# A decoder layer on one core: step order from a table of places, cross units of 4 heads by 256 tokens, and the heads' spreads, stores and broadcasts begun by SyncE

## The reference, cut to what matters

```python
x = x + attn(layernorm(x), w_qkv, w_out)          # window 128: a query chunk sees its own chunk (causal) and the one before
x = x + xattn(layernorm(x), ctx, ctx, mask, ...)  # softmax(q k^T / 4, masked) v, 77 keys for each of 4 sequences
x = x + ffn(layernorm(x), clip_x, clip_down, w_gate, w_up, w_down)   # int8-like rounding, silu(gate) * up, down
```

## Time and profile before

| | us |
|---|---|
| median of 3 runs (lowest, highest) | 945.3 (941.71, 948.7) |
| the profiled execution, its time | 945.94 |
| its span, first to last instruction | 944.2 |
| PE busy / DVE / ACT / POOL | 728.0 / 544.3 / 418.8 / 192.4 |
| granted clock of TensorE, mean | 0.866 |

### The profile page before, as it was taken

One profiled execution on the slowest core, in us unless ns is written; L12 is line 12 of the kernel. 1 busy time (PEld: TensorE's weight loads), 2 busy tenths in 40 slices (PEclk: granted clock), 3 DMA queues, 4 the chain that ended last, 5 costly groups with the idle time before them and its releaser, 6 DMA issues.

```text
span 944.2 us, 13998 instructions
## 1 busy us (share of the span) xinstructions
PE 728.0 (77%) x5008; PEld 412.4 (44%) x5008; DVE 544.3 (58%) x970; ACT 418.8 (44%) x610; POOL 192.4 (20%) x231
## 2 busy tenths in 40 slices
PE   3769888888788997989788778689795684468755
PEld 2446455555545443556445443435343221323344
DVE  4378546665854457566465753345652730559977
ACT  3414544434443544643343455132351342169865
POOL 4002121211321202110231031002002000334536
PEclk9968988899998999999898989688797565679979
DMA  8540141504221344151215413130344012000013
GB/s 258 181 134 3 51 134 42 141 14 115 70 82 30 94 104 109 48 150 48 63 47 134 98 41 86 37 108 14 86 108 130 14 40 45 0 1 1 1 45 134
DMA packets 59187, 71.78 MB, mean 76 GB/s; under 512 B 24635, under 2 KB 36079, under 8 KB 59119
## 3 DMA queue, kind: packets, MB, share of 16 engines
q1 hardware_dynamic: 43792, 50.90, 16.8%
q10 hardware_dynamic: 15327, 19.99, 10.6%
HBM read 17.74 MB, written 4.72 MB: 24 GB/s over the span
## 4 chain that ended last, share of the span: by engine, by line
PE 23%; DVE 12%; issue 6%; DMA 6%; ACT 4%; ACTq 4%; POOL 0%; SPq 0%; POOLq 0%; DVEq 0%
PE banks L676 6%; DMA oc<-sums 4%; PE banks L666 4%; ACTq L906 3%; PE banks L623 2%; PE banks L625 2%; PE banks L549 2%; DVE tops L1280 1%; PE banks L720 1%; PE banks L594 1%; DMA sums<-ls 1%; ACT big L882 1%; PE banks L596 1%; PE banks L653 1%; DVE big L1274 1%
## 5 line engine op out<-in xcount | busy, mean ns | idle before, releaser
L1109 DVE TENSOR_REDUCE mneg<-banks 128x4 f32<-128x1024 f32 (+1 forms) x128 | 145.7, 1152 | 73.8 <-PE banks L587 73.2
L1370 POOL TENSOR_SCALAR_AFFINE_SELECT big<-big 128x512 f32<-128x512 f32 x128 | 85.1, 665 | 448.3 <-ACT big L878 446.9
L878 ACT ACTIVATE big<-banks 128x1024 f32<-128x1024 f32 (+1 forms) x128 | 124.1, 973 | 107.1 <-PE banks L616 74.4
L584 PE MATMUL banks<-big 96*128 96x256 bf16 (+1 forms) x512 | 101.6, 296 | 22.2 <-DVE mneg L1109 9.1
L882 ACT ACTIVATE big<-banks 77x1024 f32<-77x1024 f32 x64 | 64.8, 1019 | 110.7 <-PE banks L625 84.6
L549 PE MATMUL banks<-xnT,weights 128*128 128x512 f32 x192 | 91.7, 607 | 3.0 <-DVE big L1082 1.2
L653 PE MATMUL banks<-big 128*17 128x256 f32 (+1 forms) x1152 | 80.1, 371 | 16.8 <-POOL big L1370 16.7
L1113 DVE TENSOR_REDUCE mneg<-banks 128x8 f32<-128x616 f32 x64 | 49.7, 793 | 68.9 <-PE banks L596 68.7
L616 PE MATMUL banks<-big 99*128 99x256 bf16 (+1 forms) x512 | 76.4, 273 | 9.7 <-ACT big L878 5.6
L587 PE MATMUL banks<-causal,identb 128*128 128x256 bf16 x256 | 77.6, 305 | 0.0
L584 PEld LDWEIGHTS banks<-big 96*128 96x128 bf16 x512 | 51.0, 109 | 58.8 <-issue 28.9
(11 more groups left out here) (150 smaller groups left out, 1165.2 us busy)
## 6 DMA issues: line engine op xcount, KB each, us to landing
big<-parts SPq DMA_DIRECT2D x288, 128.0 KB, 2.5
oc<-sums ACTq DMA_DIRECT2D x16, 512.0 KB
oTs<-oe ACTq DMA_DIRECT2D x64, 64.0 KB, 2.7
out_dram<-oTs SPq DMA_DIRECT2D x16, 256.0 KB, 2.1
xs<-in_x_dram SPq DMA_DIRECT2D x3, 1024.0 KB, 10.1
big<-oe ACTq DMA_DIRECT2D x32, 64.0 KB, 2.9
oTx<-oe ACTq DMA_DIRECT2D x32, 64.0 KB, 2.6
big<-kparts SPq DMA_DIRECT2D x96, 9.6 KB, 2.6
```

What stands on the lines that cost most here:

```text
L584: e.matmul(bank(p, j)[:, i * 256 + lo * 128:i * 256 + 256], Q[0:96, hh, c * 128:c * 128 + 128], K[0:96, hh, (c - 1 + lo) * 128:(c + 1) * 1 ...
L878: e.activation(pt[u].rearrange("p (i n) -> p i n", i=4)[:, :, 0:n], pair(p).rearrange("p j (s n) -> p (j s) n", s=2)[:, :, 0:n], ACT.Exp, ...
L1109: e.tensor_reduce(M.rearrange("p (h c) -> p h c", h=4)[:, :, c], pair(p).rearrange("p j (s n) -> p (j s) n", s=2)[:, :, lo * 128:256], AX. ...
L1370: e.affine_select(out=P[:, :, 0:128], in_=P[:, :, 0:128], compare_op=ALU.is_ge, fill=0.0, base=0, pattern=[[0, 4], [1, 128]], channel_mult ...
```

## The change

It has three parts. First, the order: `PLACE` gives for each kind of step, and for the kinds of the neighbouring jobs, the start and end of its stretch; all periods are laid on one common time line (`LENGTH`: 26.1 for an S period, 9.6 for an X period), so a step may fall into the next period. `BEHIND` gives the distances of steps that follow. Second, an X unit is now 4 heads by 256 tokens; the mask product covers two heads at once. Third, `spread` is split: `gather` (the sums) stays on ACT; the four output transfers, `store` and `widen` are begun by SP.

```diff
+LENGTH = {"s": 26.1, "x": 9.6}
+PLACE = {"max s0s": (-0.001, 0.635), "max s1s": (-0.31, 0.27), "max s1x": (-0.071, 0.513), "max x0x": (-0.04, 0.687),
...
     if k == "evac" and s[3]:
-        return ("fin", 1, ("spread", s[1], s[2]))
+        return ("fin", BEHIND["gather"], ("gather", s[1], s[2]))
+    if k == "gather":
+        return ("fin", BEHIND["spread"], ("spread", s[1], s[2]))
...
     for p in range(2 * len(JOBS)):
...
-        steps = [(-1, ("force", "rows"))] + over(-0.5, -0.1, tail)
+        put([(-0.001, ("force", "rows"))] + over(PLACE["tail " + kind], tail))
+        scores = over(PLACE["score " + kind], [("score", job, g, j) for j in range(units)])
         for j in range(units):
-            steps.append((j / units, ("score", job, g, j)))
-            if j > 1:
-                steps.append((j / units + 0.001, ("val", job, g, j - 2, False)))
-        tail = [("val", job, g, units - 2, False), ("val", job, g, units - 1, True)]
+            put([scores[j]])
+            if j >= BEHIND["val"]:
+                put([(scores[j][0] + 0.002, ("val", job, g, j - BEHIND["val"], False))])
+        tail = [("val", job, g, j, j == units - 1) for j in range(units - BEHIND["val"], units)]
         if p + 1 < 2 * len(JOBS):
-            steps += over(-0.3, 0.62, max_steps(p + 1))
+            put(over(PLACE[f"max {kind}{g}{nxt[0] if g else kind}"], max_steps(p + 1)))
...
+                elif k == "spread":
+                    _, job, g = s
+                    kind, b, f = job
+                    e.wait_ge(a_evac, n_of["evac", job, g, 1])
+                    if b:
+                        e.wait_ge(t_out, n_of["out", kind, b - 1, NC - 2])
...
                     else:
-                        blk, two = j // 2, j % 2
-                        for i in range(2):
-                            hh = 2 * two + i
-                            e.matmul(bank(p, i)[0:KX, :], xks[r][0:99, hh, :], qs[r][0:99, hh, blk * 512:blk * 512 + 512],
-                                     start=True, stop=False)
-                            t = e.matmul(bank(p, i)[0:KX, :], identb[0:KX, 0:KX], maskt[0:KX, blk * 512:blk * 512 + 512],
-                                         start=False, stop=True)
+                        keep = maskt[0:KX, j * 256:j * 256 + 256].rearrange("p (a n) -> p a n", a=1)
+                        for z in range(2):
+                            for i in range(2):
+                                e.matmul(bank(p, z)[0:KX, i * 256:i * 256 + 256], xks[r][0:99, 2 * z + i, :],
+                                         qs[r][0:99, 2 * z + i, j * 256:j * 256 + 256], start=(i == 0), stop=False,
+                                         skip_group_check=True)
+                            t = e.matmul(bank(p, z)[0:KX, :].rearrange("p (i n) -> p i n", i=2), identb[0:KX, 0:KX],
+                                         keep.to_broadcast([KX, 2, 256]), start=False, stop=True, skip_group_check=True)
...
-                        for q in range(2):
-                            i = 2 * two + q
-                            t = e.matmul(acc[:, blk][32 * i:32 * i + 17, :], xv[r][0:KX, i, 0:17],
-                                         pt[u][0:KX, q * 512:q * 512 + 512], start=True, stop=True, tile_position=(0, 32 * i))
+                        for i in range(4):
+                            t = e.matmul(acc[:, j // 2][32 * i:32 * i + 17, (j % 2) * 256:(j % 2) * 256 + 256],
+                                         xv[r][0:KX, i, 0:17], pt[u][0:KX, i * 256:i * 256 + 256], start=(j % 2 == 0),
+                                         stop=True, tile_position=(0, 32 * i), skip_group_check=True)
```

More of the change, by code:

```diff
@@ L30 @@
 HALF_AT = {"s": 3, "x": 1}
+LENGTH = {"s": 26.1, "x": 9.6}
+PLACE = {"max s0s": (-0.001, 0.635), "max s1s": (-0.31, 0.27), "max s1x": (-0.071, 0.513), "max x0x": (-0.04, 0.687),
[6 rows of a table added]
+BEHIND = {"scaled": 3, "turned": 3, "scaled 4": 0, "split": 1, "vmove": 0, "bulk": 8, "turnm": 3, "evac": 4,
+          "spread": 2, "gather": 2, "invert": 5, "store": 2, "widen": 8, "scale": 8, "wturn": 2, "val": 2}
 def follow(s):
@@ L102, in run, with over @@
             self.put(s)
-def over(start, end, steps):
-    return [(start + (end - start) * i / len(steps), step) for i, step in enumerate(steps)]
+def over(span, steps):
+    return [(span[0] + (span[1] - span[0]) * i / len(steps), step) for i, step in enumerate(steps)]
 def stats_steps(kind, b):
@@ L159, in attention_order, with put @@
     tail, normed = [], {("s", 0)}
+    timed, start = [], 0.0
+    def put(steps):
+        timed.extend(((start + t * length, len(timed) + i, step) for i, (t, step) in enumerate(steps)))
     for p in range(2 * len(JOBS)):
@@ L181, in attention_order @@
-            if last[2] == 1 and (job[0] == "s" or last[0] == "x"):
-                steps += over(0.7 if job[0] == "s" else 0.9, 1.0, out_steps(*last[0:2]))
+            if nxt:
+                put(over(PLACE["bulk " + kind], [("bulk", nxt, 1, z) for z in range(2)]))
+                if nxt[0] == "s":
+                    put(over(PLACE["v " + kind], [("v", nxt, c0) for c0 in (0, 4)]))
+                else:
+                    put(over(PLACE["keys " + kind], [("xkeys", nxt), ("bulk", nxt, 0, 1)]))
@@ L189, in attention_order @@
             if n + 2 < len(JOBS):
-                steps += over(0.08, 0.7, [("force", "norm")] + qk_steps(JOBS[n + 2]))
+                put(over(PLACE["qk " + kind], [("force", "norm")] + qk_steps(JOBS[n + 2])) + [(0.98, ("force", "proj"))])
             if last == ("x", last[1], 1):
-                steps += over(0.05, 1.0, third_steps(last[1]))
+                put(over(PLACE["third " + kind], third_steps(last[1])))
         if p in fw_at:
-            steps += over(0.2, 1.0, fw[slice(*fw_at[p])])
@@ L195, in attention_order @@
-        o.run([s for _, s in sorted(steps, key=lambda it: it[0])] + ([("force", "proj")] if g else []))
+            put(over((0.2, 0.97), fw[slice(*fw_at[p])]))
+        start += length
+    o.run([s for _, _, s in sorted(timed, key=lambda it: it[0:2])])
     o.run(tail)
```

91 lines of the change are left out of this document (42 added, 49 removed), and 6 rows, old and new, of the table PLACE.

## The result

The changed kernel takes **871.75 us** (median; 865.81 to 885.96), the one before in the same job 945.19. The ratio is 0.920, with a 95% interval from 0.914 to 0.927. The forecast was 910, and the range ended at 872, so the direction was right and the size half of what came.

A forecast was written before the change was run, and what follows sets the result against it. PE was taken to bound the stage, busy 595.4 of 714.4 us. The terms −15 −12 −9 −6 +12 +3 −1 −8 sum to −36 us, from 945.9 to 910 us; the range was 872 to 946.

The forecast's parts named there:

- the clock: PE's granted clock rises as its idle share falls, by the slope between two windows; −8 us (0 to −25).
- ACT's queue: 128 transfers and 32 of `store` and `widen` leave ACT, so exponentials behind them wait less; −9 us (0 to −20).
- chain: Transfers behind a job, up to `out`, now begun by SP: some jobs wait longer, some less; +3 us (−10 to +25).
- end: At the very end of the kernel, the reciprocal and four `spread` transfers overlap on two queues; −1 us.
- Cross `val`: Cross `val` steps of 4 heads by 256 tokens take less PE time in 16 periods; −15 us (−8 to −18).
- The tail: More matmuls between an S group's last `score` and last `val` steps cover exponential and selection; −12 us (−6 to −16).
- Cross keys: Keys of X2a are begun a period earlier, behind fewer transfers, cutting an 8.0 us wait; −6 us (−2 to −8).
- `turnm` to the first `score`: Matmul work covering the maxima's copy and transfer falls short in 12 groups instead of 6; +12 us (+5 to +18).
- More gaps close: Rival: evenly spread steps also cut `turnm` waits and raise the late clock; another −15 and −25, 870 us; chance 0.15.
- The first rival: The rival "More gaps close": 870 us, chance 0.15.
- The second rival: PE waits as much as before, elsewhere; only cross `val` and part of the clock's gain stay; 940 us, chance 0.12.
- SP holds the chain: Rival: a waiting `bulk` in SP's in-order list delays `spread`, `store`, `widen` and what follows; 970 us, chance 0.10.

## Why the prediction was right and wrong

Three steps failed. The gain of the clock was taken from the slope between two windows, −8, and was −33.5. The waits were taken from the single largest line of a releaser, or at nothing where DVE's maxima were concerned, −12, and were −36. And the move to SyncE was priced apart from the order, at −7 in all (ACT's queue, chain and end), where it gave 42 us in the new order and costs 48 in the old. By term:

**Cross `val`, −15: right by itself, less in the sum.** Alone the X unit gives 14.6 us (in its stage content −12.4, clock's cost −8.3, idle time +12.2, so the number is in part the clock's). Instead of 256 records with a median of 604 ns there are 512 with 391, and four heads lie side by side (ns shortest/median/longest):

```profile
L712 PE MATMUL banks<-big x512: 379/391/634, 312.3 to 709.8; 77*17 77x256 f32 x171
```

In the changed kernel the content fell by 8.9 only. All 64 X `val` steps together have a content of 48.0 us before and 34.7 after, each counted up to the start of what follows, so 13.3 less. But the new order splits `val` steps into more runs (139 to 167), and each run costs about 0.21 us more than steps of one kind would (below), 6 us: a term that I left out. In the new order alone the content rises by 5.0 us. The added matmuls of `score` cost nothing, as taken:

```profile
302.54 0.38 PE L673 MATMUL banks<-maskt,identb 77*77 77x512 bf16 x1
302.76 0.38 PE L670 MATMUL banks<-big 99*77 99x256 bf16 x2
302.98 0.38 PE L673 MATMUL banks<-maskt,identb 77*77 77x512 bf16 x1
```

Two of 256 columns start 0.22 us ahead of what follows (302.76 to 302.98), and so does one of 512 (302.54 to 302.76). The Trainium skill's about 60 cycles for each matmul (TensorEngine Tiling (Array Packing), Instruction Overhead) would, by an estimate from that figure, add 0.025 us for the second of two; this trace does not show it.

**The tail, −12: right.** 16.7 to 2.0 us of waits (I had left 4), and 14.5 to 19 us by its own run, the clock's part with it.

**ACT's queue, −9 (0 to −20): mis-sized.** The waits for exponentials were 19.3 us in the stage, on seven lines of which I had read one,'s 4.7. They fell by 18.6. Only 7.7 of that came with the move in the new order (8.4 to 0.7), near the −9; 11 had gone with the order alone, by a way for which the sum had no term.

**Cross keys, −6: wrong.** The wait of X2a went, two others came (4.80 and 4.23), since the keys of a cross job in an S period stand behind `store`. It might have been worth little anyway: in the run with early keys a later wait ended at nearly the same time, and the kernel was not faster.

**`turnm` to the first `score`, +12: right.** 3.5 to 17.3 us, +13.8. The largest, 7.26 us, is the weights' loading, not the short distance.

**The chain, +3: near in size, wrong in mechanism.** 20.3 to 19.6, and the last job's 13.9 to 13.3. I had the new order neutral and SyncE as the slower way. It is the other way round: with the transfers on ACT the `out` waits grew to 31.5 in the new order, and the move took 12 of them back. That the number came near is luck. Without the later output places they are 66.5.

**The maxima of `rows`: no term.** 25.3 to 9.5, −15.8, nearly all of it with the order alone (11.1). I had it as the rival "More gaps close", with −15, and gave it 0.15.

**The clock, −8 (0 to −25): mis-sized**, −33.5. The slope between two windows did not carry. Idle time fell from 18.2% to 14.8% of the stage, and clock and idle time do not go together from kernel to kernel: order and X unit on ACT have 114.1 us of idle time and 73.9 of clock's cost, the move in the old order 194.3 and 61.0, the one with both waits removed 102.3 and 55.2. The runs place the gain, since it came with the move in the new order, but do not say why. Even in one kernel the clock differs between executions: 865.81 us at 0.907, 873.37 at 0.888. A forecast of this term needs bounds of some 30 us, not one number.

**The sum.** Idle time −36 where the sum had −12; clock −33.5 for −8; content −9 for −15; around it −1.5. The first rival's 870 us was met with its mechanism (waits at `turnm`; clock of the late window 0.77 to 0.85, of the first 0.92 to 0.97, together −33.5 where it had −8 −25). That it lands within 5 us is luck in part: what cross `val` and keys fell short of, ACT's exponentials and DVE's maxima of scores made up. The second rival's 940 has a +9 for which the prediction gives no term. "SP holds the chain" was no idle thought either: it is what happens with the same move in the old order, 48 us, two fifths of them shown to come by the way that I described, with DVE's maxima behind `scale`. I had not asked whether the new order was what kept it away, so I priced the move and the order apart: alone they are worth −48 and 27 us, and both with the X unit 75.

## What to carry to other kernels

When a change moves work to another queue and reorders it at once, price the pair: a queue in order is fast or slow by what stands in front, and here the same move was worth −48 or +42 us. A wait removed in front of a chain that ends later may be worth nothing; look for the next wait before counting it, and read all lines of one releaser, not the largest. Give the clock's part wide bounds. And compare the order in which a queue's transfers begin, in both traces, before a run about that order is read: one edit here left it as it was.

## What the runs showed of the hardware that I had not expected

- Column groups have a price at their edges. From the first matmul of an S `score` step to the next step it takes 0.44 us if a `score` or `max` follows and 0.53 if `val` does; from `val` (4 heads in 4 column groups) to the next step 0.56 instead of 0.44. That is 0.09 and 0.12 us for each run of `val` steps, worked out from such steps at 2.4 GHz with no idle time in them.
- A transfer of row maxima, issued at 647.68 between five loads of some 2 MB (645.72 to 648.74), held PE for 7.26 us; the other eight waits for such transfers are 10.0 us in all. With the loads later it was 1.95 us. The issue and the wait in the changed kernel:

```profile
647.68 0.78 ACTq L915 DMA_DIRECT2D big<-m3t  x1
...
655.98 0.62 PE L670 MATMUL banks<-big 99*77 99x256 bf16 x2 [7.26 <-DMA big<-m3t]
```

- PE's clock rises with what PE does, useful or not (0.866 to 0.906 with idle work in the kernel before). Neither kernel with idle work was faster for it, but in both the idle work was longer than the idle time it took, so what the clock alone is worth was not measured.
- The clock's cost can fall by half with little change of idle time: 73.9 to 36.7 us when the transfers moved to SyncE in the new order, with idle time 114.1 to 96.6. What in PE's work made the difference is open.
